# One pool of three banks for the first pass and the turns, and the values of two key blocks together, in the third layer's attention heads

## The reference

```
q = hidden_states @ Wq.T
k = hidden_states @ Wk.T
v = hidden_states @ Wv.T
...
q = q * cos + rotate_half(q) * sin
k = k * cos + rotate_half(k) * sin
...
scale = 1.0 / jnp.sqrt(jnp.float32(HEAD_DIM))
scores = jnp.einsum('bhqd,bhkd->bhqk', q, k) * scale
attn = jnp.einsum('bhqk,bhkd->bhqd', jax.nn.softmax(scores, axis=-1), v)
```

## Time and profile before

| | us |
|---|---|
| median of 3 runs | 3993.09 |
| lowest, highest | 3988.18, 3993.31 |
| the profiled execution | 3988.51 |
| its span | 3986.7 |
| PE busy | 3548.5 (89%) |
| DVE busy | 2353.9 (59%) |
| ACT busy | 1557.1 (39%) |
| first pass, 512 matmuls (L1658) | 180.1 |
| second pass, 512 matmuls (L1668) | 187.2 |
| values, 2048 instructions (L1680) | 162.1 |
| reads of the first pass, 512 (L1747) | 329.5 |
| exponentials, 256 (L1734) | 261.9 |

### The profile page before, as it was taken

How to read it: one execution, slowest core, us unless ns; L and a number is a source line. 1 busy time by engine, 2 the same in 40 slices (tenths; PEclk the granted TensorE clock), 3 DMA queues, 4 the chain that set the end, 5 groups by cost and what they waited for, 6 DMA issues and landing times. The chain is left out here.

```text
span 3986.7 us, 65977 instructions
## 1 busy us (share of the span) xinstructions
PE 3548.5 (89%) x21608; PEld 2615.5 (66%) x21608; DVE 2353.9 (59%) x4783; ACT 1557.1 (39%) x2820; POOL 1383.1 (35%) x1085
## 2 busy tenths in 40 slices
PE   6899999999797999999986599999699997999576
PEld 4777777777575888888862344444388856886354
DVE  3555555655423656666655677775477746776444
ACT  2444444444333444444432246664233333333111
POOL 1333333333133666666643200000133352335144
PEclk8999999999898999999998889999799998999755
DMA  0000000000001000000002311221233303331144
GB/s 33 7 5 3 5 5 5 3 5 5 32 0 43 18 18 17 17 17 17 17 0 74 121 74 75 76 75 40 64 93 105 98 15 101 93 104 49 58 107 96
DMA packets 115990, 178.66 MB, mean 45 GB/s; under 512 B 22288, under 2 KB 65040, under 8 KB 115600
## 3 DMA queue, kind: packets, MB, share of 16 engines
q1 hardware_dynamic: 109776, 169.38, 13.8%
q0 software_dynamic: 6144, 8.39, 1.3%
HBM read 151.51 MB, written 25.95 MB: 45 GB/s over the span
## 5 line engine op out<-in xcount | busy, mean ns | idle before, releaser
L424 POOL TENSOR_TENSOR l0h_probs<-l0h_probs,l0h_inv 128x128 f32<-128x128 f32 (+7 forms) x256 | 292.8, 1146 | 585.7 <-DVE l0h_inv L459 585.7
L1747 DVE TENSOR_REDUCE l2h_half<-l2h_s 128x1 f32<-128x512 f32 x512 | 329.5, 685 | 94.9 <-PE l2h_s L1658 94.9
L1734 ACT ACTIVATE l2h_PT<-l2h_s 128x1024 f32<-128x1024 f32 x256 | 261.9, 1023 | 194.9 <-PE l2h_s L1668 194.6
L355 PE MATMUL l0h_sc<-l0a_KT,l0h_QT 128*128 x768 | 296.8, 499 | 30.0 <-ACT l0h_probs L528 28.4
L382 PE MATMUL l0h_cx<-l0h_PT,l0h_VG 128*128 128x128 f32 x2304 | 300.7, 276 | 0.0
L528 ACT ACTIVATE l0h_probs<-l0h_sc,l0h_negtop 128x128 f32<-128x128 f32 (+7 forms) x256 | 189.7, 741 | 245.3 <-DVE l0h_negtop L454 244.9
L382 PEld LDWEIGHTS l0h_cx<-l0h_PT,l0h_VG 128*128 128x128 f32 x2304 | 278.0, 192 | 1.0
L159 POOL TENSOR_TENSOR XN<-XN,n_rstd 128x512 f32<-128x512 f32 x32 | 39.9, 1266 | 633.6 <-DVE n_rstd L140 633.6
L1658 PE MATMUL l2h_s<-l2h_K,l2h_Q 128*128 128x512 f32 x512 | 180.1, 428 | 22.5 <-DMA l2h_K<-l_split 18.8
L452 DVE TENSOR_REDUCE l0h_top<-l0h_sc 128x1 f32<-128x128 f32 (+7 forms) x256 | 194.0, 758 | 8.8
L355 PEld LDWEIGHTS l0h_sc<-l0a_KT,l0h_QT 128*128 128x128 f32 x768 | 125.6, 192 | 106.6 <-issue 63.7
(11 more groups left out here) (408 smaller groups left out, 8869.8 us busy)
## 6 DMA issues: line engine op xcount, KB each, us to landing
l3p_decb<-l_decays SPq DMA_DIRECT2D x128, 256.0 KB, 4.2
l3p_w<-L_w SPq DMA_DIRECT2D x34, 512.0 KB, 3.7
l2h_Q<-l_split SPq DMA_DIRECT2D x64, 256.0 KB
l2h_K<-l_split SPq DMA_DIRECT2D x64, 256.0 KB
l3p_prow<-l_decays SPq DMA_DIRECT2D x128, 128.0 KB, 3.0
l_split<-l2q_hi SPq DMA_DIRECT2D x16, 512.0 KB, 3.8
l_split<-l2q_lo SPq DMA_DIRECT2D x16, 512.0 KB, 3.8
mx_wgu<-L_ffn_w_gate_up SPq DMA_DIRECT2D x32, 256.0 KB
```

What stands on the lines that cost most here:

```text
L355: mm = pe.matmul(sc[u % 2][:, lo:lo + n], QT[:, u * P:(u + 1) * P], KT[:, ds(g, 1), b * S + lo:b * S + lo + n], start=True, stop=True)
L424: pool.tensor_tensor(p, p, inv[:, u % 4:u % 4 + 1].to_broadcast([P, keys(u)]), ALU.mult).then_inc(probs_scaled, 1)
L1734: act.activation(PT[:, b, kb, :], s2[kb % 2][:, :], ACT.Exp, scale=L2_SCALE).then_inc(exped, 1)
L1747: dve.reduce_max(half[:, b, t, z:z + 1], s1[i % 2][:, :], AX_X).then_inc(maxed, 1)
```

## The change

Three things, all in `l2_heads`.

1. The bank `turns` is dissolved. The first pass has three banks, and the 16 pieces, the turn of the maxima and the turn of the context share them in 18 slots a pair, slot s in bank s mod 3. The maxima are turned in slot 2 and the context in slot 7. One semaphore, `s1_read`, counts every read that sets a bank free (16 maxima, the split, the normalisation) in the order of slots, in place of `maxed`, `m_ready` and `ctx_kept`. Whoever writes a slot waits for the read of the slot three before.
2. PE's order in a step is by pairs of key blocks: first-pass piece, second pass, piece, second pass, (the turn of the maxima in the first pair, of the context in the second), two pieces, then the values of both blocks.
3. DVE's order follows: pieces 0 and 1, split, pieces 2 to 5, normalise, pieces 6 to 15, top.

What each engine computes is the same. The diff, cut to its core:

```
--- before.py
+++ after.py
@@ -1550,19 +1550,20 @@
         mhi, mlo = st.sb("mhi", [NQ, 2, P], F32R), st.sb("mlo", [NQ, 2, P], F32R)
         inv = st.sb("inv", [P, 4, 2])
         VH = st.sb("VH", [P, 2, NQ, L2_W])
-        s1 = [st.ps(f"s1_{i}") for i in range(2)]
+        s1 = [st.ps(f"s1_{i}") for i in range(3)]
         s2 = [st.ps(f"s2_{i}", 2 * BANK) for i in range(2)]
-        turns, pv = st.ps("turns"), st.ps("pv")
+        pv = st.ps("pv")
         ctxT = st.sb("ctxT", [P, 2 * P])
-        pmt = turns[0:NQ, NQ * L2_W:NQ * L2_W + P]
...
         NP = 2 * NQ
-        TURN_AT = 1
+        TOP_AT, CTX_AT = 2, 6
+        TOP_SLOT, CTX_SLOT, SLOTS = TOP_AT, CTX_AT + 1, NP + 2
+        READ_BY_LAST = SLOTS * (L2_N - 2) + 31
         MROW = SPLIT
 
         def steps(engine, step):
@@ -1589,6 +1590,21 @@
 
             return not isinstance(h, int) or B * h + b + n < L2_N
 
+        def slot_of(i):
+            return i + (i >= TOP_AT) + (i >= CTX_AT)
+
+        def bank(slot):
+            return s1[slot % 3]
+
+        def read_ahead(n):
+            if isinstance(n, int) and n < 2:
+                return {-2: 0, -1: NP, 0: 2 * NP + 1, 1: 3 * NP + 2}[n]
+            return SLOTS * n + 31
+
+        def read_up_to(n, slot):
+            missing = () if not isinstance(n, int) or n >= 2 else (TOP_SLOT, CTX_SLOT) if n == -2 else (CTX_SLOT,)
+            return read_ahead(n) + slot + 1 - sum(m <= slot for m in missing)
+
         with nc.Block() as block:
 
             @block.sync
@@ -1608,9 +1624,12 @@
                     sp.sem_inc(second_loads, 1)
                     load(Q2[:, b, :], K2[:, b, :], h, b, q2_loaded[b])
 
+                def top_read(n):
+                    return READ_BY_LAST + 1 if isinstance(n, int) and n == L2_N - 1 else read_up_to(n - 1, TOP_SLOT)
+
                 def load_max(h, b):
                     n = B * h + b
-                    sp.wait_ge(m_ready, n + 1)
+                    sp.wait_ge(s1_read, top_read(n))
                     for i, m in enumerate((mhi, mlo)):
                         sp.dma_start(Q2[MROW + i:MROW + i + 1, b, :].bitcast(F32).rearrange("a (t n) -> a t n", t=NQ), m[:, b, :].bitcast(F32)).then_inc(m_loaded[b], 16)
 
@@ -1654,8 +1673,8 @@
                         t, z = divmod(i, 2)
                         if i == 0:
                             pe.wait_ge(q1_loaded[b], 32 * h + 32)
-                        wait(pe, maxed, NP * n + i - 1)
-                        pe.matmul(s1[i % 2][:, :], Q1[:, b, t * P:(t + 1) * P], K1[:, b, z * BANK:(z + 1) * BANK],
+                        wait(pe, s1_read, read_up_to(n - 2, slot_of(i) - 3))
+                        pe.matmul(bank(slot_of(i))[:, :], Q1[:, b, t * P:(t + 1) * P], K1[:, b, z * BANK:(z + 1) * BANK],
                                   start=True, stop=True).then_inc(s1_made, 1)
 
                 def second_pass(h, b, kb):
@@ -1682,38 +1701,47 @@
                     if kb == NQ - 1:
                         mm.then_inc(pv_made, 1)
 
-                def turn(m, ctx, top_of):
-
-                    wait(pe, m_ready, min(m, L2_N) if isinstance(m, int) else m)
-                    if ctx:
-                        pe.wait_ge(pv_kept, m - 2)
-                        wait(pe, ctx_kept, m - 3)
+                def turn_top(n, of, read):
+                    pe.wait_ge(top_ready, n + 1)
+                    pe.wait_ge(s1_read, read)
+                    pe.transpose(bank(TOP_SLOT)[0:NQ, 0:P], top[:, of, :], k.ident[:, :]).then_inc(top_turned, 1)
+
+                def turn_ctx(j, read):
+                    pe.wait_ge(pv_kept, j + 1)
+                    pe.wait_ge(s1_read, read)
+                    for i in range(2):
+                        mm = pe.transpose(bank(CTX_SLOT)[:, i * P:(i + 1) * P], ctxT[:, i * P:(i + 1) * P], k.ident[:, :])
+                    mm.then_inc(ctx_turned, 1)
+
+                first_pass(0, 0, range(NP))
+                first_pass(0, 1, range(TOP_AT))
+                turn_top(0, 0, read_up_to(-1, TOP_SLOT - 3))
+                first_pass(0, 1, range(TOP_AT, NP))
+
+                def step(h, b):
+                    n = B * h + b
+                    for kb in range(0, NQ, 2):
                         for i in range(2):
-                            mm = pe.transpose(turns[:, i * P:(i + 1) * P], ctxT[:, i * P:(i + 1) * P], k.ident[:, :])
-                    if top_of is not None:
-                        pe.wait_ge(top_ready, m + 1)
-                        mm = pe.transpose(pmt, top[:, top_of, :], k.ident[:, :])
-                    mm.then_inc(turned, 1)
-
-                first_pass(0, 0, range(NP))
-                turn(0, False, 0)
-                first_pass(0, 1, range(NP))
-
-                def step(h, b):
-                    for kb in range(NQ):
-                        second_pass(h, b, kb)
+                            if exists(h, b, 2):
+                                first_pass(*after(h, b, 2), (2 * kb + i,))
+                            second_pass(h, b, kb + i)
+                        if kb == 0:
+                            if exists(h, b, 1):
+                                turn_top(n + 1, 1 - b, READ_BY_LAST if not exists(h, b, 2) else read_up_to(n, TOP_SLOT - 3))
+                        if kb == 2:
+                            if not isinstance(h, int) or h > 0:
+                                turn_ctx(n - 2, READ_BY_LAST + 2 * b if not exists(h, b, 2) else read_up_to(n, CTX_SLOT - 3))
                         if exists(h, b, 2):
-                            first_pass(*after(h, b, 2), range(2 * kb, 2 * kb + 2))
-                        if kb == TURN_AT:
-                            turn(B * h + b + 1, not isinstance(h, int) or h > 0, (b + 1) % B if exists(h, b, 1) else None)
+                            first_pass(*after(h, b, 2), (2 * kb + 2, 2 * kb + 3))
                         if not is_first(h, b):
-                            values(*before(h, b), kb)
+                            for i in range(2):
+                                values(*before(h, b), kb + i)
 
                 steps(pe, step)
-                turn(L2_N + 1, True, None)
+                turn_ctx(L2_N - 2, READ_BY_LAST + 3)
                 for kb in range(NQ):
                     values(L2_HEADS - 1, B - 1, kb)
-                turn(L2_N + 2, True, None)
+                turn_ctx(L2_N - 1, READ_BY_LAST + 4)
 
             @block.scalar
             def _(act):
@@ -1721,7 +1749,7 @@
                     n = B * h + b
                     act.wait_ge(pv_made, n + 1)
                     if not is_first(h, b):
-                        act.wait_ge(turned, n + 3)
+                        act.wait_ge(ctx_turned, n)
                     act.activation(ctxT[:, :], pv[:, 0:2 * P], ACT.Copy).then_inc(pv_kept, 1)
 
                 def step(h, b):
@@ -1744,49 +1772,52 @@
                     for i in pieces:
                         t, z = divmod(i, 2)
                         dve.wait_ge(s1_made, NP * n + i + 1)
-                        dve.reduce_max(half[:, b, t, z:z + 1], s1[i % 2][:, :], AX_X).then_inc(maxed, 1)
+                        dve.reduce_max(half[:, b, t, z:z + 1], bank(slot_of(i))[:, :], AX_X).then_inc(s1_read, 1)
 
                 def take_top(h, b):
                     n = B * h + b
-                    dve.wait_ge(maxed, NP * (n + 1))
+                    dve.wait_ge(s1_read, read_up_to(n - 2, SLOTS - 1))
                     dve.reduce_max(top[:, b, :], half[:, b, :, :], AX_X).then_inc(top_ready, 1)
 
                 def split_max(h, b):
                     n = B * h + b
-                    dve.wait_ge(turned, n + 1)
+                    pmt = bank(TOP_SLOT)[0:NQ, 0:P]
+                    dve.wait_ge(top_turned, n + 1)
                     wait(dve, m_loaded[b], 32 * h)
                     dve.tensor_copy(mhi[:, b, :], pmt).then_inc(mhi_ready, 1)
                     dve.wait_ge(mhi_ready, n + 1)
-                    dve.tensor_tensor(mlo[:, b, :], pmt, mhi[:, b, :].bitcast(F32), ALU.subtract).then_inc(m_ready, 1)
+                    dve.tensor_tensor(mlo[:, b, :], pmt, mhi[:, b, :].bitcast(F32), ALU.subtract).then_inc(s1_read, 1)
 
                 def normalise(h, b):
                     n = B * h + b
 
-                    out = turns[:, 0:NQ * L2_W].rearrange("p (i g e) -> p g i e", i=2, e=L2_W)
-                    dve.wait_ge(turned, n + 4)
+                    out = bank(CTX_SLOT)[:, 0:NQ * L2_W].rearrange("p (i g e) -> p g i e", i=2, e=L2_W)
+                    dve.wait_ge(ctx_turned, n + 1)
                     dve.reciprocal(inv[:, :, :], out[:, :, :, L2_HD]).then_inc(inv_ready, 1)
                     dve.wait_ge(inv_ready, n + 1)
                     dve.tensor_tensor(CT[:, b * NQ:(b + 1) * NQ, ds(h * L2_HD, L2_HD)].rearrange("p (g i) e -> p g i e", i=2), out[:, :, :, 0:L2_HD],
-                                      inv[:, :, :].unsqueeze(3).to_broadcast([P, 4, 2, L2_HD]), ALU.mult).then_inc(ctx_kept, 1)
```

(26 more changed lines are left out.)

## The result

| | before | after |
|---|---|---|
| median of 4 runs, us | 3992.14 (3988.18 to 3993.31) | 3953.89 (3952.78 to 3955.61) |
| the profiled execution, its span | 3988.51, 3986.7 | 3955.61, 3953.8 |

The ratio is 0.9906, 95% interval 0.9889 to 0.9923: 38 us or 0.94% faster. The prediction was 3948, range 3937 to 3975. The mean step is 12.96 where 12.8 was forecast, and one part of it has another cause: the forecast put the turns at 0.44 and a wait for VectorE (DVE) at 0.1; in their place stands a wait for DVE, with what it makes late behind it, of 0.72 a step, and the turns lie inside it. The letters are those of the prediction: F a first-pass matmul, S one of the second pass, V the values of a key block, T and C the turns of the maxima and of the context.

What follows compares the result with a forecast made beforehand. TensorE was taken to bound the stage: 12.2 + 0.44 + 0.1 gave 12.7, with long loads 12.8 a step for 14.12, 38 us over 29 steps; start 3 and end 2 made 43 off, written as 3948, range 3937 to 3975.

Steps and rivals of the forecast that it cites:

- Joining the values, 1.4 a step: TensorE's key-block pairs: one way into V and out of it instead of two, 3.05 a pair for 3.40.
- Rival B: Joining the values saves nothing, since next weights load under the running matmul; only 8 us gained, 3985; chance 11%.
- F to S free: TensorE's order within a pair: changing from F to S costs nothing extra, as in the first step.
- Rival C: Slower: each new change from F to S costs 0.35, a step takes 15.5, 4029 us; chance 4%.
- The turns, 0.44: The three transposes on TensorE, now standing apart, cost between 0.30 and 0.68 a step; 0.44 taken.
- the stall of 0.1 at F 7: F 7 wants its weights at 4.9, its bank's reader ends at 5.0: 0.1 a step, due to VectorE.
- The walk over the slots: Timing of the 18 bank slots of a step by read durations; only F 7 found late, by 0.1.
- Rival D: One semaphore in slot order lets one late reader hold every F, 0.2 a turn: 3960 us; chance 8%.
- The third bank: F waits for the slot three before, not two: 0.16 a step goes, and the start gains 3 us.
- Loads allow 12.3, 0.1 added for long streams: SP's loads permit a step of 12.3, 0.4 under TensorE's 12.7; longer streams add 0.1 to the mean, 12.8.
- rival A: The loads hold every step at 13.3, so 28 us gained, 3965; sign: DMA waits over 10 us; chance 17%.
- Start 3 and end 2: Gains of 3 us in the F ahead of the first S, and 2 us in the last two steps.

Runs made afterwards that it cites:

- the banks alone: Three first-pass banks with 18 slots as in the change, but TensorE's old order block by block, against the kernel before: 3983.91 us, ratio 0.9973.
- wide loads: The change with each Q or K load going over its 16 rows of a head first: 3949.24 us, ratio 0.9883 to the kernel before.
- the run with the turns at the head: The change with the turns moved to the start of the second and third pairs (slots 4 and 9): 3947.38 us, ratio 0.9880 to the kernel before.

## Why the prediction was right, and where not

**Joining the values, 1.4 a step: right.** With the values apart the step is 1.39 longer, and pairs without a turn are 3.04 to 3.07. Rival B (weights of the next form load under the running matmul, so that joining saves nothing) is refuted; the Trainium skill (TensorE: Matmul & The Clock Gate, Part 2, first step) agrees with the trace between F and S and not at V.

**F to S free: right.** S rows behind F are 0.62 or 0.63. Rival C is refuted.

**The turns, 0.44, and the stall of 0.1 at F 7: the step that failed.** Together 0.54, measured 0.36 + 0.36 = 0.72. The turns cost 0.3 together with the banks alone and 0.2 at the head of a pair, both less than 0.44, and in the change they lie inside the wait. The walk over the slots named F 7 but not the last F of the pair with T, as it let a read begin 0.43 after its F and last 0.64. By these figures two reads end at 0.43 + 1.28 = 1.71, just under the 1.72 at which the last F is due. Two things are off in it. Behind V the pair's first F is read 0.54 after its start (2541.66, 2542.20), and its second F starts 0.81 after it (2542.47). And 0.64 is the time per read of a stretch in which reads overlap; one read by itself lasts 0.69. The page before has both, 329.5 / 512 = 0.64 and 685 ns:

```profile
L1747 DVE TENSOR_REDUCE l2h_half<-l2h_s 128x1 f32<-128x512 f32 x512 | 329.5, 685 | 94.9 <-PE l2h_s L1658 94.9
```

So the second read ends at 0.54 + 1.39 = 1.93, and the last F starts at 1.98. An error of 0.2 in a wait that was taken to be just avoided shows in full; and the 0.11 by which V is late behind a late F was in no term. Of the forecast, this is 0.18 x 29 = 5 us. That it is no more is in part luck: 0.44 had been booked for turns that cost 0.2 to 0.3, and the excess covers a part of the wait that was missed.

**Rival D** (0.2 a turn from a late reader on the one semaphore) is no farther off in size than the forecast: the step is 0.09 a turn over it, and the measured 3954 lies midway between 3948 and D's 3960. The number alone would not tell the two apart. But its cause is not the one: the F that waits waits for its own bank's read, and with the same one semaphore the waits go when the turns change slots.

**The third bank: undervalued.** The prediction gave it 0.16 a step and the start, and did not say that the joining rests on it. With two banks the order gains nothing that can be told (0.9993), the banks without the order 0.27%, both together 0.94%. Three quarters of the gain need both.

**Loads allow 12.3, 0.1 added for long streams: right in kind.** The issue is 1.48 ahead of S (2540.52, 2542.00), the usual stream 11.3. PE's waits for a load inside steps 1 to 29 come to 0.4 us in all, far under the 10 of rival A. The mean lies 0.05 over the regular step, and less than that is the loads', as the long step 1 stays with wide loads. That 12.3 is close to the bound was seen only in the run with the turns at the head, whose steps want 12.38 and are held at 12.61. A regular step of 12.91 is at the upper end of the 12.6 to 12.9 that the prediction asked for.

**Start 3 and end 2: 2.6 and 2.5.** At the start the first F of step 0 waits for its load in the profile after, a wait that I had booked only as a smaller gain:

```profile
2322.53 0.79 PE L1677 MATMUL l2h_s<-l2h_K,l2h_Q 128*128 128x512 f32 x1 [2.02 <-DMA l2h_K<-l_split]
```

## What to carry to other kernels

An order that saves changes of form on TensorE packs the producers closer, and its saving can be paid back to the last digit as a wait for a bank: count the banks with the order, as here the order was worth nothing without the third bank. When a slot walk says "just in time", take the length of one read and not the time per read of a busy stretch (0.69 and 0.61 to 0.64 here), let each read begin from where its own matmul starts, and add the weight load that a late matmul exposes. Where one engine is full and the one it feeds is at nine tenths, grouping work of the first can starve the second: here two V in a row paid and four in a row lost all of it.

## What the runs showed of the hardware that was not expected

- A matmul that comes late for a bank costs more than its wait: V starts 0.43 behind such an F, 0.32 behind one whose weights were already in.
- One read of a bank of 128 x 512 by DVE lasts 0.67 to 0.69 in every trace, but reads that find their banks ready start 0.60 apart and overlap (six in 3.68). A bank is free only after the whole of its read.
- The loads ran at 94 GB/s with a DMA share of 0.24, and with the 16 rows as the outer index at 208 GB/s and 0.93, the same bytes in the same 256 packets of 4 KB a step. So nearly four times the share of the engines brought 2.2 times the rate. The Trainium skill (DMA: Bandwidth & Descriptors, Why a DMA increments its semaphore by 16 and not by 1) says that a transfer is spread over the largest number of engines up to 16 that divides the slowest dimension of both sides: by it 4 before, of the four pieces, and 16 with the rows first. The trace agrees, 0.24 being about 4 engines of 16 and 0.93 nearly all. Neither the first-pass reads nor PE's regular step changed beside the denser traffic.
